# Decoder layer with mixer, cross attention and top-2 experts: a third batch joins the sorted expert tiles

## The reference

```python
def _sinkhorn(log_alpha, iters=3):
    for _ in range(iters):
        log_alpha = log_alpha - logsumexp(log_alpha, axis=-1, keepdims=True)   # over the 8 experts
        log_alpha = log_alpha - logsumexp(log_alpha, axis=-2, keepdims=True)   # over the 512 tokens
    gates = exp(log_alpha)
    return gates / (sum(gates, axis=-1, keepdims=True) + 1e-08)

def _ffn(x, router_w, router_b, temperature, wg, wp, wo):                      # x: layer norm of x2
    gates = _sinkhorn((x @ router_w.T + router_b) / maximum(temperature, 0.1))
    topk_vals, topk_idx = top_k(gates, 2)
    topk_gates = topk_vals / (sum(topk_vals, axis=-1, keepdims=True) + 1e-08)
    g = relu(einsum('btd,edf->btef', x, wg)); p = einsum('btd,edf->btef', x, wp)
    all_out = einsum('btef,efd->bted', g * p, wo)                              # 8 experts, FF = 256
    return x + sum(take(all_out, topk_idx) * topk_gates)

x = x + mixer(layernorm(x))
x = x + cross_attention(layernorm(x), ctx)
x = x + _ffn(layernorm(x), ...)
```

## Time and profile before

| | before |
|---|---|
| median of 3 runs | 407.91 us (406.83 to 408.59) |
| profiled execution | 405.84 us |
| its span | 404.0 us |
| mean granted clock of TensorE | 0.893 of full speed |
| TensorE busy | 325.1 us (80%) |
| VectorE busy | 243.6 us (60%) |
| ScalarE busy | 149.6 us (37%) |
| GpSimd busy | 145.9 us (36%) |
| chain that ended last | PE 50%, DVE 23%, issue 9%, POOL 7%, DMA 5%, ACT 4% |

### The profile page before, as it was taken

How to read it: one execution, slowest core, us unless ns; L and a number is a source line. 1 busy time by engine, 2 the same in 40 slices (tenths; PEclk the granted TensorE clock), 3 DMA queues, 4 the chain that set the end, 5 groups by cost and what they waited for, 6 DMA issues and landing times.

```text
span 404.0 us, 5655 instructions
## 1 busy us (share of the span) xinstructions
PE 325.1 (80%) x1775; PEld 206.9 (51%) x1775; DVE 243.6 (60%) x681; ACT 149.6 (37%) x298; POOL 145.9 (36%) x179
## 2 busy tenths in 40 slices
PE   1455668669997989978987589837989899899995
PEld 1333345344454624544444344325877677588883
DVE  6586375864199651696249882115556379977662
ACT  2403404625645145414442143502546421332331
POOL 7332213382022050002003127700364683566663
PEclk9985695959999989999899598965899999999999
DMA  4302770241003336024301001342100621342000
GB/s 105 79 1 57 176 233 1 72 91 50 2 0 80 83 101 99 3 75 98 90 0 54 1 7 52 109 106 74 33 20 25 182 95 38 101 146 85 11 0 26
DMA packets 31401, 26.86 MB, mean 66 GB/s; under 512 B 5856, under 2 KB 28066, under 8 KB 31157
## 3 DMA queue, kind: packets, MB, share of 16 engines
q1 hardware_dynamic: 30125, 24.40, 23.7%
q0 software_dynamic: 1248, 2.11, 1.6%
HBM read 19.53 MB, written 7.23 MB: 66 GB/s over the span
## 4 chain that ended last, share of the span: by engine, by line
PE 50%; DVE 23%; issue 9%; POOL 7%; DMA 5%; ACT 4%; SPq 2%; POOLq 0%; DVEq 0%; ACTq 0%
DVE nmax_mask L1283 6%; PE pC L1714 3%; PE pS L328 3%; PE pC L1711 3%; PE pS L1479 3%; POOL sort_scr L743 3%; PE pS L329 2%; PE pS L330 2%; PE pS L1476 2%; PE pS L1667 2%; PE pS L1534 2%; PE pS L1670 2%; PE pG L1451 2%; DMA q_stack<-sort_scr 1%; POOL out_scr L760 1%
## 5 line engine op out<-in xcount | busy, mean ns | idle before, releaser
L1283 DVE TENSOR_REDUCE nmax_mask<-pS 128x3 f32<-128x462 f32 (+1 forms) x96 | 52.4, 576 | 16.8 <-PE pS L1670 16.4
L906 ACT ACTIVATE prob<-pS 128x512 f32<-128x512 f32 x80 | 43.8, 596 | 23.2 <-PE pS L1485 13.4
L1667 PE MATMUL pS<-k_stack,q_stack 72*128 72x154 bf16 x256 | 36.0, 246 | 3.3 <-DMA q_stack<-q_scr 3.2
L781 POOL TENSOR_TENSOR xi_lo<-late,xi_hi 128x512 fp32r<-128x512 f32 x22 | 28.7, 1304 | 20.6 <-ACT xi_hi L966 20.5
L1670 PE MATMUL pS<-mbias,ident_bf 128*128 128x462 bf16 (+1 forms) x96 | 35.1, 366 | 0.0
L760 POOL DMA_INDIRECT out_scr<-expert_y,meta x23 | 22.7, 985 | 20.3 <-ACT expert_y L955 15.6
L1667 PEld LDWEIGHTS pS<-k_stack,q_stack 72*128 72x128 bf16 x256 | 21.6, 106 | 11.4 <-issue 5.7
L1664 PE MATMUL pS<-mbiasT,ident_bf 128*128 128x128 bf16 x72 | 17.4, 242 | 12.1 <-DVE nmax_mask L1283 12.1
L966 ACT CAST xi_hi<-late 128x512 fp32r<-128x512 f32 x22 | 13.7, 621 | 36.3 <-DVE late L1339 36.3
L786 POOL TENSOR_SCALAR ffn_veps<-ffn_mv 128x4 f32<-128x4 f32 x4 | 0.9, 226 | 71.2 <-DVE ffn_mv L1218 71.2
L1476 PE MATMUL pS<-q_stack,k_stack 75*128 75x512 bf16 (+1 forms) x64 | 24.7, 386 | 1.0 <-ACT prob L906 1.0
(11 more groups left out here) (397 smaller groups left out, 841.6 us busy)
## 6 DMA issues: line engine op xcount, KB each, us to landing
prob<-w_scr SPq DMA_DIRECT2D x16, 256.0 KB, 3.4
q_stack<-q_scr SPq DMA_DIRECT2D x9, 384.0 KB
q_scr<-q_parts SPq DMA_DIRECT2D x12, 128.0 KB, 2.4
k_stack<-k_scr SPq DMA_DIRECT2D x36, 40.0 KB
sort_scr<-blank SPq DMA_DIRECT2D x5, 258.0 KB, 6.0
q_stack<-sort_scr SPq DMA_DIRECT2D x5, 258.0 KB, 2.8
res<-in_x_dram SPq DMA_DIRECT2D x4, 256.0 KB, 4.8
prob<-in_L_ffn_wg_dram SPq DMA_DIRECT2D x1, 1024.0 KB, 6.0
```

The source lines that it names most:

```text
L781: pool.tensor_tensor(hid_lo[u % NHID], hid[:, u % 2, :], f32(hid_hi[u % NHID]), ALU.subtract).then_inc(s_hidlo, 1)
L906: act.activation(prob[:, (NSB * b + n) % NBUF, :], score_bank(b, NSA + n)[:, :], ACT.Exp).then_inc(s_exp, 1)
L1283: dve.tensor_reduce(nmax[:, qt, hs[0]:hs[-1] + 1], score_bank(b, n)[:, 0:len(hs) * KEYS].rearrange("p (h k) -> p h k", k=KEYS), AX.X, ALU. ...
L1667: pe.matmul(dst[:, i * KEYS:(i + 1) * KEYS], q_stack[b % 2][0:STACK, h, qt * P:(qt + 1) * P], k_stack[b % 2][0:STACK, h, 0:KEYS], start=(i ...
```

## The change

Batch 2 becomes a second sorted group (NSORT = 2). Batches 0 and 1 leave the last tile of each expert part-filled; such a tile is now an *open* tile, one for each expert, with the fixed numbers OPEN to OPEN + 7 = 24 to 31. Batch 2's rows first fill the open tile of their expert and then spill into whole tiles. `place_picks` gets, beside the start of an expert (base), the row from which its picks go elsewhere (limit) and how far (jump). Tiles 0 to 8 (FIRST = 9) can only hold rows of batches 0 and 1; the expert of tiles 9 to 23 is known once batch 2 is placed, that of the open tiles always. NT goes from 23 to 32 tiles (8 chunks, 16 pairs) and UNITS from 32 to 16. The loads of chunks 2 and on wait for batch 2's 8 scatters, tile 9 waits for the expert numbers.

To have batch 2's gates in time, its tail moves from the table POST_AT (slots 12 to 35 of batch 3) to POST2_AT (7 to 21), its whole router group from the tiles into slots 23 to 41 of batch 3 (ROUTER1_AT, now with rank, place and scatter), and router group 2 (batch 3) into tiles 13 to 29. TensorE's first step of a group's column maximum waits for the column sums of the group before instead of for a copy. Combine runs for three batches.

The raw expert weights no longer lie in prob but in the place of the low parts (wgp_raw shares the memory of wgp_lo; the subtraction is in place). They are loaded in slot 29 of batch 1 and split in slots 1 to 19 of batch 2; the exponentials wait for them no longer.

```diff
     GB = GRP[0][1]
-    DENSE0 = GB
+    NSORT = 2
+    DENSE0 = sum(nb for _, nb in GRP[:NSORT])
     PICKS = 2
-    NT = (PICKS * GB * S + E * (P - 1)) // P
+    FIRST = -((E * (P - 1) - PICKS * GB * S) // P)
+    OPEN = PICKS * DENSE0 * S // P
+    NT = OPEN + E
...
-        wgp = [sb("wgp_hi", [P, E, 2, FF], F32R), sb("wgp_lo", [P, E, 2, FF], F32R)]
+        with nc.sbuf_tensor("wgp_raw", [P, E, 2, FF], F32) as wgp_raw:
+            pass
+        wgp_lo = sb("wgp_lo", [P, E, 2, FF], F32R)
+        wgp = [sb("wgp_hi", [P, E, 2, FF], F32R), wgp_lo]
...
-        EXPERTS_AT = [17, 18, 19, 20, 21, 22, 23, 24]
+        LOAD_EXPERTS_AT = 29
+        EXPERTS_AT = [1, 1, 4, 10, 13, 13, 16, 19]
...
+        POST2_AT = [7, 7, 8, 9, 10, 12, 12, 13, 14, 14, 17, 21, 21]
...
+        ROUTER1_AT = [23, 24, 25, 25, 25, 25, 27, 27, 28, 28, 29, 30, 30, 32, 33, 33, 34, 35, 36, 39, 40, 41, 41, 41,
+              41, 41, 41]
...
-            if grp > 0:
+            if grp >= NSORT:
                 return steps + [("gates_T", grp, 0)]
...
-            if b == 0:
+            if b == 2:
                 place([("split_experts", 0, n) for n in range(EXPERT_STEPS)], EXPERTS_AT)
...
-                place(post(b - 1), POST_AT)
+                place(post(b - 1), POST_AT if b + 1 < NB else POST2_AT)
...
                 place(router(0)[len(ROUTER_AT[0]):], ROUTER_AT[1])
+                place(router(1), ROUTER1_AT)
...
                 elif step == "load_rows":
 
                     t0, nt = CHUNKS[b]
-                    sp.wait_ge(s_in, 16 * PICKS * T * GB)
+                    sp.wait_ge(s_in[0], 16 * PICKS * T * GB)
+                    if t0 + nt > FIRST:
+                        sp.wait_ge(s_in[1], 16 * PICKS * T)
...
                     before = NSB * b + n - NBUF
                     if before >= 0:
                         act.wait_ge(s_pv, before // 5 + 1)
-                    else:
-                        act.wait_ge(s_wsplit, EXPERT_STEPS)
...
+            def place_picks(g, part):
...
                     if g == 0:
...
+                        dve.tensor_tensor(jump[:, :], open_row[:, :], last_row[:, 0, :], ALU.subtract)
...
+                    else:
+                        step(dve.tensor_tensor(count[:, :], picked_n, filled[:, :], ALU.add))
+                        step(dve.tensor_scalar(spill[:, :], count[:, :], 1, 1, ALU.max, ALU.subtract))
+                        step(dve.tensor_scalar(spill[:, :], spill[:, :], -P, None, ALU.bitwise_and))
...
+                    step(dve.tensor_tensor(over, rank, wide_rows(limit), ALU.is_ge))
+                    dve.tensor_tensor(slot, rank, wide_rows(base), ALU.add)
+                    step(dve.tensor_tensor(at, over, wide_rows(jump), ALU.mult))
+                    step(dve.tensor_tensor(slot, slot, at, ALU.add))
+                    step(dve.tensor_tensor(at, slot, mask_bf[g][:, :, :], ALU.mult))
...
-                        pe.wait_ge(s_wrow, b - 1)
+                        pe.wait_ge(s_colsum, SINKHORN_ITERS * b)
...
-                        pe.wait_ge(s_pos, NAMED)
-                    experts[b] = pe.value_load(tile_expert[0:1, b:b + 1], min_val=0, max_val=E - 1)
+                    if b in (0, FIRST):
+                        pe.wait_ge(s_named, 1 if b == 0 else NSORT)
+                    experts[b] = (pe.value_load(tile_expert[0:1, b:b + 1], min_val=0, max_val=E - 1) if b < OPEN
+                                  else b - OPEN)
```

More of the change, by code:

```diff
@@ new lines, in build_decoder @@
+        last_row = sb("last_row", [P, NSORT, E])
+        pick_at = [by_sort("pick_at%d_" % k, []) for k in range(PICKS)]
+        pick_sum = by_sort("pick_sum", [])
+        pick_row = [by_sort("pick_row%d_" % k, [], I32) for k in range(PICKS)]
+        pick_w = [by_sort("pick_w%d_" % k, []) for k in range(PICKS)]
+        past_n = sb("past_n", [1, OPEN], I32)
+        tile_expert = sb("tile_expert", [1, OPEN], I32)
+        rows01 = late[:, :].rearrange("p (k n c) -> p k n c", k=PICKS, c=ROW)
@@ L307, in build_decoder @@
                              "picked_in", "combined"))
+        s_in = [sem("rows_scattered%d" % g) for g in range(NSORT)]
         s_back = [sem("tile_outputs_scattered%d" % i) for i in range(2)]
@@ L415, in router @@
             steps += [("gates", grp, 0), ("gates", grp, 1), ("gates", grp, 2)]
-            if grp > 0:
+            if grp >= NSORT:
                 return steps + [("gates_T", grp, 0)]
             return steps + [("rank", grp, 0)] + [("place", grp, i) for i in range(4)] + [
-                ("scatter", grp, i) for i in range(GB)]
+                ("scatter", grp, i) for i in range(GRP[grp][1])]
         def post(b):
@@ L1110, in combine @@
+                        step(dve.tensor_reduce(pick_w[k][g][:, :], tie, AX.X, ALU.add))
+            pos_steps = [0]
             def combine(b, k):
```

272 lines of the change are left out of this document (146 added, 126 removed).

## The result

The first four runs of the changed kernel have a median of 381.15 us (375.32 to 381.95) beside 407.86 us (406.83 to 408.59) for before: ratio 0.9266, 95% interval 0.9155 to 0.9376. Ratios are made without runs of a slower state, here the two of 381.95 us, so they can differ from the quotient of the medians. Six more runs gave 379.78 us (379.13 to 380.45) beside 405.6 us, ratio 0.9374, interval 0.9327 to 0.9420. The forecast was 383.5, with a range of 376 to 395. The first profiled execution of the changed kernel was among its longest (381.95 us), so this part reads the second one (380.12 us, span 378.4 us).

A forecast was written before the change was run, and what follows sets the result against it. VectorE was taken to bound batch 3's first half, TensorE its second half, the tiles and the dense stage. Terms A to F sum to -24.4 us on the 404.0 us span: 379.6, profiled 381.4, median 383.5 (range 376 to 395).

The forecast's parts named there:

- F: Dense stage, from unit 0 to the end: one dense batch instead of two, 44.8 us for 80.0, -35.2 (-38 to -30).
- A: Batch 0: splitting of expert weights leaves, ending ScalarE copies and GpSimd collisions, with some clock regained: -5.5 us (-7.5 to -2).
- B: Batch 2's first half: the expert-weight splitting arrives there, beside VectorE's work: +0.5 us (0 to +3).
- C: Batch 3's first half: batch 2's tail adds VectorE work, 4.5 us, and two GpSimd collisions, 2: +6.5 (+3 to +10).
- D: Batch 3's second half to the first tile: GpSimd's scatters start earlier and run without the residual: -2.4 us (-4 to +5).
- TensorE's new wait: Batch 3's second half: TensorE waits for the first column sum of batch 2's router, put at 3.5 us.
- so that both chains end together: Batch 3's second half: TensorE's 3.5 us wait plus slow matmuls make its chain end with GpSimd's.
- E: Tile stage: 32 tiles for 23, 63.5 us instead of 51.8, +11.7 (+7 to +20).
- I keep their 16.5 us: Tile stage: the first six tiles were taken to last 16.5 us as before, at a mean clock of 0.57.
- rival 2: Tiles run bare: batch 3's router hides and tiles take 1.41 us each, -7, 376.5 us; chance 0.08.
- the low clock through the tiles: Rival: TensorE stays at 1.2 GHz for all 25 further tiles, +26.5, 410.0 us; chance 0.03.
- rival 1: Batch 3 pays more: a column-sum wait of 6 us and four collisions, +7, 390.5 us; chance 0.20.

The follow-up runs named there:

- e7_router_later: The kernel before, with batch 2's router group three tiles later among the tiles and batch 3's logits two later: 408.67 us, ratio to before 1.0049.
- e3_tail_early: The kernel before, with only batch 2's tail moved to slots 7 to 21 of batch 3, and the splits of w_o with it: 412.78 us, ratio 1.0162.
- e5_rows_first: The changed kernel, with loads of the first two chunks of sorted rows ahead of w_o's load on SyncE: 376.91 us, ratio to before 0.9295.
- e4_shift_first: The changed kernel, with batch 2's router steps ahead of the placing of batches 0 and 1 in batch 3: 380.07 us, ratio to before 0.9393.

## Why the prediction came out right, and where it did not

**The sign and the size** rested on F, and F held: -37.4 us for -35.2. One dense batch went (32 gates became 16), and of the 4.4 us of stalls that I carried over as 3.2 only 0.8 were left: from VectorE's first gate at 336.83 to the sixteenth at 369.44 are 32.61 us, against 31.8 without a stall. Four of the six bursts of combining lay between the gates and hid; two lay behind the last gate, from which it was 8.95 us to the end for 8.8.

**A** was right in its mechanism and its largest part. Splitting the maxima takes 1.26 us for 4.23, -3.0 of the 3.3 forecast (its first cast still takes 0.51 us beside a GpSimd subtraction); the part ahead of it, with ScalarE's copies, gave 0.85 of 1.1; and TensorE's transposes then followed its own work and took 0.3 us of this back. The 1.1 us for the clock did not come: over the 30.1 us that the earlier trace rows has at 0.83, counted from the copy of the maxima, the clock is 0.83 again. (Most of that stretch is batch 0's second half. The first half had 0.76 before and has 0.74.) The stretch to batch 1's copy is 0.95 us longer (a like trace of the kernel before, in e7_router_later, has 51.8 us there too, so that is spread). The first 47 us, unchanged in both, varied from 47.4 to 49.2 us over the traces. **B** was nothing.

**C** came out at +8.3 for +6.5. Its mechanism was right in kind: two more collisions did come, four for two, but they added 0.8 us and not 2, and with the tail's instructions (4.8 us by the prediction's own terms, where it writes 4.5) VectorE's busy time rose by 4.9. What the sum put at nothing were waits: 3.4 us more of idle time, 1.9 of it for the logits from TensorE, which was at 1.2 GHz there. The view was read as if VectorE alone bounded this half. And 1.2 of the 8.3 us lie behind VectorE's last part of the maxima: TensorE was still at the scores before its transposes, and the copy came 1.70 us after the parts for 0.50. In e3_tail_early, with the tail alone, it was +7.1.

**D** is the step that failed: +2.0 for -2.4. Forecast and found: the residual no longer splits the scatters (they took 1.2 us less), and TensorE's new wait is there, 2.23 us for 3.5.

```profile
247.25 0.64 PE L1838 MATMUL pT<-route_gate,all_ones 128*128 128x32 f32 x2 [2.23 <-ACT route_gate L1007]
```

Wrong: that the scatters would start 1.1 us earlier. They start 5.38 us after the copy, as before, and by the prediction's own count, from the maxima's parts, 7.1 us after (240.05 to 247.13), where 5.9 was measured before and 4.7 forecast; from the parts D is +3.2 and not +2.0. The mis-sized term is the trip to TensorE: beside eighteen instructions of 0.2 us the 4.7 us leave about 1 us for it, and VectorE's wait in it alone was twice that:

```profile
242.88 0.28 DVE L1452 TENSOR_REDUCE ecol_max<-pT 8x1 f32<-8x128 f32 x1 [2.03 <-PE pT L1824]
```

The transpose of the column maxima stands behind the late copy of the maxima. The row numbers were ready 6.2 us after the parts, and the first scatter began 0.9 us later still. And wrong in the sentence "so that both chains end together", as if that were free: TensorE's end releases w_o's load, which then lay on the rows (6.94 us for 2.77). That was not in the sum, and e5_rows_first prices it at 2.9 us. It depends on which chain ends first: with TensorE 3 us ahead w_o cost a little over 1 us on the last scatters, with TensorE a little ahead (e4_shift_first) it was 4.6 us on the last scatter, with both together it was 4.2 us on the rows.

**E** came out at +3.75 for +11.7, below its bound of +7. (That bound was mis-added: bare pace is 16.5 + 25 x 1.41 + 4.7 = 56.5 us, which is +4.7.) "I keep their 16.5 us" was the error: the first six tiles of before held ten steps of batch 2's router, among them the trip to TensorE with its wait, and these left with the change. They took 10.15 us, and e7_router_later shows the same six at 11.3 us with five of the ten steps left in them by its table and the trip moved out. (Those five, and batch 3's tail, which is a little later in the changed kernel, can account for the 1.2 us between the two; that was not run.) The rest was sized well: 45.39 us to unit 0, where the sum has 47.0 (42.3 and the 4.7 of the end); the 25 tiles took 1.64 us each with their steps, not the 1.41 of rival 2. A cost that was carried over as belonging to a place belonged to the steps that lay there.

So the forecast was near (383.5 for 381.15 and 379.78) by luck, through errors of opposite sign: E 8 us too high, C, D, A and B with the start 9 us too low, F 2 too high. The sign and the rough size were not luck, since F outweighs all of these. Of the rivals, the low clock through the tiles did not come (1.00 from the seventh tile on); the higher price of batch 3 (rival 1) did, 6 us over C and D, and was outweighed.

## What to carry to other kernels

When a stage is carried over from a trace, take out first what the change takes out of it: its time per unit holds the steps of others. A wait behind another engine's queue is a term of the sum, also where the instructions are small. When two chains are made to end together, list what the end of each releases, the transfers above all, and see what they would then lie on. A transfer that nobody needs soon belongs behind the one that somebody waits for, on the same queue.

## What was not expected of the hardware

TensorE stayed at 1.2 GHz for 34 us (223.2 to 257.3), although it was busy 12.32 of 18 and 12.93 of 16 us there; with one more product of 512 columns in each slot it was granted 0.81 of full speed in the first of these stretches, and the time hardly moved. And a VectorE cast with a single input in SBUF (m_parts<-m_r) was stretched to 1.15 us beside GpSimd's subtractions, as the two-input instructions around it were; in batch 3 a one-input instruction of 128x8 elements (rcol_inv, L1063) took 0.63 us for 0.17. The Trainium skill, SBUF — State Buffer, section Who interferes with whom, excepts one-input instructions outside the two-port modes, and counts casts and tensor_scalar among those that can enter such a mode; in which mode these two ran no run here shows.
